# Two cross attentions on one core: one stored row for an item's columns and keys, and norms stored by item

## The chip, the core and the metric

The kernel runs on 1 core of a Trainium2 chip. Its engines, each with its own instruction stream, are PE (TensorE), DVE (VectorE), ACT (ScalarE), POOL (GpSimd) and SP, which here only issues transfers. The transfers of all streams run on 16 DMA engines. The metric is the device time in microseconds (us) of one execution, start to end; before and after are compared by the medians of several runs.

## The reference, cut to what matters

Two layers work on `x` (64 items of 32 rows of 256); each is a cross attention, a self attention and a mixture of experts, each added to `x`. Both cross attentions read the same context `ctx_1024` (64 items of 257 keys of 128). The second one normalizes queries and keys:

```
def _L1_xattn_ref(hidden_states, encoder_hidden_states, Wq, Wk, Wv, Wo, gq, gk):
    ...
    q = rmsnorm(q, gq)
    k = rmsnorm(k, gk)
    scores = jnp.einsum('bqhd,bkhd->bhqk', q, k) * scale
    attn = jax.nn.softmax(scores, axis=-1)
    out = jnp.einsum('bhqk,bkhd->bqhd', attn, v)
    out = out.reshape(B, Sq, H * D)
    return out @ Wo
```

There are 16 heads of 128. The norm of a key differs by head and key, so for an item it is 16 x 257 numbers.

## The kernel before

The stages follow each other, each in its own block: `begin`, `cross_attention` with layer 0 (some 60 to 580 us of the profile), `self_attention`, `routed_experts` (made of `route`, `experts` and `bridge`, up to some 1375 us), `cross_attention` with layer 1 (to some 2230 us), then the second layer's self attention and experts.

**Cross attention.** The weights of queries and keys are folded, so that an item's scores are one product of `qT` with the item's context columns (`ctxT`, context turned to 128 x 257), and the mix is a product of the probabilities with the context rows (`keys`, 2 blocks of 128 keys), from which the item's last, 257th key has been subtracted (`last_key`), since its share follows from the others. An outer iteration covers 8 items (`NB`), each 4 steps (`R`) of 4 heads; there are 8 iterations. In step s PE turns the probabilities of step s, makes the scores of step s+4 (`AHEAD`) and mixes step s-3 (`LAG`). DVE multiplies scores by `key_scale` and takes the maximum (L750), makes `shift` (L754), and divides by the sum (L765, L766); ACT takes the exponential (L637) and keeps the turned probabilities (L645). Between iterations PE makes the next queries.

**Layer 0** loads the rows of an item 8 items ahead (`ROWS`), POOL subtracts the last key (`less_last`, L891) into a ring of 4 (`RING`), and PE turns the rows into `ctxT`, which stays on the chip.

**The norms of the keys** (`KeyNorms`) are made beside `route`, `experts` and `bridge`: PE multiplies 128 keys at a time by the key weights, ACT and DVE sum squares, and groups of 512 keys are turned and stored in the DRAM tensor `rk`, a row of 16448 + 512 numbers for each head, four copies. In `experts` ACT issues these stores, in `bridge` SP. `route` also stores `ctxT` in the DRAM tensor `ctx_cols`, in 8 pieces, since its place on the chip is needed.

**Layer 1** takes for each item: the columns (L431), the keys (L432), the last key copied to all partitions (L434), and the scales in 4 transfers, one for each step (L440). `columns`, `keys` and `last_key` are rings of 4, filled when the item four before is mixed; `key_scale` has two buffers. All these are issued by SP in the order in which they are written, so a wait holds up what stands behind it. The wait before L440 lets the load for item b go when item b-2 has been scored. POOL subtracts the last key here too, then issues 16 gathers (L947) in four quarters at items 3 to 6: rows of the experts' output that DVE adds to `x` in the next iteration (`take`, L783). Between the first and the second quarter stands `norm_scale` (L871, L872), which makes `rstd` for the next iteration; DVE's `normalize` (L717), which stands right behind the first score of item 5, waits for it. After each of the first four iterations SP issues three loads of codes (L1997) for the following self attention, before the last iteration 16 loads of scales (L2007).

## Time and profile before

| | us |
|---|---|
| median of 3 runs | 3126.5 |
| lowest and highest | 3115.49 and 3131.35 |
| the profiled execution, its own time | 3116.77 |
| its span, first to last instruction | 3115.0 |
| PE busy | 2820.8 (91%) |
| DVE, ACT, POOL busy | 1478.4, 1352.8, 743.7 |
| mean granted PE clock | 0.957 |

The profile is one execution; its times are taken from the span's start. PE is the busiest engine. A busy share over the whole span mixes stages with different limits, so it is read by stretch. Registers, waits and issues of transfers don't count as busy. A wait is put down to what came last before the instruction started.

### The profile page before, as it was taken

How to read it: one execution, taken by the hardware profiler on the slowest of the kernel's cores; microseconds unless marked ns; L12 is line 12 of the kernel's file. 1: busy time of each engine (PE TensorE's matmuls, PEld its weight loads, DVE VectorE, ACT ScalarE, POOL GpSimd, SP SyncE). 2: the span in 40 equal slices, each digit the busy share in tenths (PEclk: the TensorE clock that was granted, in tenths of full speed). 3: DMA queues.
4: the chain of work that ended last, by engine and by line, in shares of the span. 5: the costliest groups of instructions: out<-in, count | busy, mean ns of one | idle time of the engine just before them, and what ended most of it. 6: DMA issues, size and time to landing. Idle time of an engine off the chain costs nothing. (4 is left out here: it accounts for less than half of the span.)

```text
span 3115.0 us, 50339 instructions
## 1 busy us (share of the span) xinstructions
PE 2820.8 (91%) x13964; PEld 2112.3 (68%) x13964; DVE 1478.4 (47%) x4967; ACT 1352.8 (43%) x4875; POOL 743.7 (24%) x948
## 2 busy tenths in 40 slices
PE   6999999798999899867887887798799999997999
PEld 5888888686444444345664665566678888885888
DVE  3665556465776444435435534543433333332333
ACT  2555455465666566524334334433422222221333
POOL 1332223263555000233322313223320000000000
PEclk9999999899999999988988999999899999998999
DMA  4110000202500243125246335525520000000000
GB/s 151 29 28 23 20 23 13 84 0 94 197 2 1 87 119 109 45 69 132 55 96 124 73 77 101 104 55 109 127 62 0 0 0 0 0 0 27 7 10 10
DMA packets 190907, 176.28 MB, mean 57 GB/s; under 512 B 32348, under 2 KB 171033, under 8 KB 189107
## 3 DMA queue, kind: packets, MB, share of 16 engines
q1 hardware_dynamic: 167762, 143.95, 16.3%
q0 software_dynamic: 14592, 27.33, 5.5%
q10 hardware_dynamic: 8416, 3.57, 0.8%
q8 instruction: 39, 0.64, 0.1%
q14 instruction: 98, 0.79, 0.1%
HBM read 147.41 MB, written 39.90 MB: 60 GB/s over the span
## 5 line engine op out<-in xcount | busy, mean ns | idle before, releaser
L529 PE MATMUL xa_mix_ps<-xa_probsT,xa_keys 128*128 128x256 f32 x1024 | 322.0, 399 | 0.0
L509 PE MATMUL xa_score_ps<-xa_columns,xa_qT 128*128 128x257 f32 x512 | 183.8, 449 | 96.1 <-DVE xa_shift L754 73.6
L637 ACT ACTIVATE xa_probs<-xa_probs,xa_shift,xa_row_scale 128x257 f32<-128x257 f32 x256 | 153.7, 601 | 269.2 <-DVE xa_shift L754 243.1
L221 PE MATMUL rt_kn_key_ps<-moe_w_wk,all_big 128*128 128x512 f32 x560 | 253.4, 605 | 7.3 <-remote 4.6
L2084 PE MATMUL sa_work_ps<-sa_xnT,all_big 128*128 128x128 f32 x2048 | 237.0, 279 | 11.2 <-ACT sa_xnT L2154 5.7
L516 PE MATMUL xa_probsT_ps<-all_ident,xa_probs 128*128 128x128 f32 x1024 | 209.7, 288 | 40.4 <-ACT xa_probsT L645 17.4
L2084 PEld LDWEIGHTS sa_work_ps<-sa_xnT,all_big 128*128 128x128 f32 x2048 | 235.3, 196 | 12.0 <-ACT sa_xnT L2154 6.1
L496 PE MATMUL xa_misc_ps<-xa_xnT,cross_folded 128*128 128x256 f32 x1024 | 232.9, 382 | 6.2 <-ACT xa_squares L622 5.6
L645 ACT ACTIVATE xa_probsT<-xa_probsT_ps 128x256 f32<-128x256 f32 x512 | 188.4, 370 | 93.6 <-PE xa_probsT_ps L516 82.8
L538 PE MATMUL xa_misc_ps<-cross_folded,xa_mixT 128*128 128x256 f32 x1024 | 228.2, 379 | 0.0
L529 PEld LDWEIGHTS xa_mix_ps<-xa_probsT,xa_keys 128*128 128x128 f32 x1024 | 202.6, 203 | 29.7
L516 PEld LDWEIGHTS xa_probsT_ps<-all_ident,xa_probs 128*128 128x128 f32 x1024 | 137.9, 147 | 124.5 <-DVE xa_probs L766 49.0
L496 PEld LDWEIGHTS xa_misc_ps<-xa_xnT,cross_folded 128*128 128x128 f32 x1024 | 194.9, 191 | 39.6 <-ACT xa_squares L622 12.2
L538 PEld LDWEIGHTS xa_misc_ps<-cross_folded,xa_mixT 128*128 128x128 f32 x1024 | 194.6, 190 | 26.5
L766 DVE TENSOR_SCALAR xa_probs<-xa_probs,xa_share 128x257 f32<-128x257 f32 x512 | 198.6, 388 | 18.2
L221 PE MATMUL ex_kn_key_ps<-moe_w_wk,all_big 128*128 128x512 f32 x448 | 202.1, 594 | 0.7 <-DVE moe_kn_stats L270 0.7
L750 DVE CUSTOM_DVE_ANT_0 xa_probs<-xa_score_ps,xa_key_scale 128x257 f32<-128x257 f32 x256 | 107.9, 422 | 183.3 <-DMA xa_key_scale<-rk 77.9
L221 PEld LDWEIGHTS rt_kn_key_ps<-moe_w_wk,all_big 128*128 128x128 f32 x560 | 104.8, 193 | 130.6 <-issue 110.9
L242 ACT ACTIVATE rt_kn_key_ps<-rt_kn_key_ps 128x128 f32<-128x128 f32 x560 | 148.3, 265 | 91.9 <-PE rt_kn_key_ps L221 65.8
L637 ACT ACTIVATE xa_probs<-xa_probs,xa_top 128x257 f32<-128x257 f32 x256 | 130.0, 508 | 106.7 <-DVE xa_top L750 103.7
L509 PEld LDWEIGHTS xa_score_ps<-xa_columns,xa_qT 128*128 128x128 f32 x512 | 89.6, 214 | 122.2 <-DVE xa_shift L754 94.8
L509 PE MATMUL xa_score_ps<-all_big,all_spare 128*128 (+1 forms) x512 | 152.6, 385 | 1.4 <-issue 0.8
(309 smaller groups left out, 5241.8 us busy)
## 6 DMA issues: line engine op xcount, KB each, us to landing
xa_key_scale<-rk SPq DMA_DIRECT2D x256, 128.5 KB
ctx_cols<-all_big SPq DMA_DIRECT2D x8, 1028.0 KB
xa_columns<-ctx_cols SPq DMA_DIRECT2D x64, 128.5 KB
xa_rows<-in_ctx_dram SPq DMA_DIRECT2D x64, 128.0 KB, 2.2
xa_last_key<-in_ctx_dram SPq DMA_DIRECT2D x128, 64.0 KB, 3.0
xa_keys<-in_ctx_dram SPq DMA_DIRECT2D x64, 128.0 KB
cross_folded<-in_L_ffn_w_gate_dram SPq DMA_DIRECT2D x32, 192.0 KB, 2.5
cross_folded<-in_L_ffn_w_up_dram SPq DMA_DIRECT2D x32, 192.0 KB, 2.7
```

Of the source, the lines that this page charges most:

```text
L221: pe.matmul(self.key_ps[m % self.banks][0:n, :], self.ctxT[:, c * P:c * P + n], self.wk[:, q * 512:(q + 1) * 512], start=True, stop=True). ...
L242: ins = act.activation(keys, keys, ACT.Square, accum_out=self.sums[0:n, c, q * self.HQ + h:q * self.HQ + h + 1])
L496: ins = pe.matmul(misc_ps[hp % 2][:, j * N:(j + 1) * N], folded[:, 2 * hp + j, c * P:(c + 1) * P], xnT[:, c, :], start=(c == 0), stop=(c = ...
L509: pe.matmul(score_ps[s % 2][:, 0:S2], qT[:, b, r * HR:(r + 1) * HR, :].rearrange("p h t -> p (h t)"), columns[:, b % RING, :] if layer els ...
L516: ins = pe.transpose(probsT_ps[s % 2][:, k * P:(k + 1) * P], probs[:, s % SR, k * P:(k + 1) * P], ident[:, :])
L529: ins = pe.matmul(mix_ps[b % 2][:, cols], keys[:, b % RING, k, :], probsT[:, b % 2, k, cols], start=(k == 0), stop=(k == KB - 1))
L538: ins = pe.matmul(misc_ps[t][:, 0:D], mixT[:, h, t * P:(t + 1) * P], folded[:, h, NC * P:FOLDED], start=(h == 0), stop=(h == H - 1))
L637: act.activation(probs[:, s % SR, :], probs[:, s % SR, :], ACT.Exp, bias=least, scale=scale, accum_out=total[:, col]).then_inc(exped, 1)
L645: act.activation(probsT[:, b % 2, :, r * P:(r + 1) * P], probsT_ps[s % 2][:, 0:KB * P].rearrange("p (k n) -> p k n", k=KB), ACT.Copy).then ...
L750: ins = dve.tensor_tensor_reduce(out=probs[:, s % SR, :], in0=score_ps[s % 2][:, 0:S2], in1=other, scale=1.0, scalar=start, op0=op, op1=pi ...
L766: dve.tensor_scalar(probs[:, s % SR, :], probs[:, s % SR, :], share[:, col], None, ALU.mult).then_inc(probs_ready, 1)
L2084: ins = pe.matmul(ps[:, j, :], w[:, c, h * HD:(h + 1) * HD], xnT[:, c, :], start=(c == 0), stop=(c == NC - 1))
```

## The change

In layer 0 SP also stores, for each item, its columns and its keys less the last in one row for each partition of a new DRAM tensor `pairs` (513 numbers, 2052 B). Layer 1 loads that row in one transfer into a ring `pair`, of which `columns` and `keys` are parts; POOL's subtraction there, `last_key` and `ctx_cols` go. The tensor `rk` is laid out by item, copy, head and key; heads are ordered so that the 4 heads which a block of 32 partitions needs follow each other, and L440 becomes 4 loads of 32 partitions with rows of 4 x 257 numbers (4112 B). A group of 512 keys belongs to up to 3 items, so its store becomes up to 3 transfers: 77 in `experts` instead of 26, 19 in `bridge` instead of 7. In layer 1, POOL waits before each quarter of the gathers until the items before it are mixed. The loads of codes move from behind an iteration's 8 items to behind its items 1, 3 and 5.

```
-RK_AHEAD = GROUP
 RK_COPIES = 4
+PAIR = S2 + (S2 - 1) // P * DC
...
+    def parts(self, j):
+
+        a, b = self.groups[j]
+        start, stop = a * P, min(b * P, KEYS)
+        return [(item, max(start, item * S2), min(stop, (item + 1) * S2)) for item in range(start // S2, (stop - 1) // S2 + 1)]
+
+    def stores_to(self, j):
+
+        return sum(len(self.parts(k)) for k in range(j % 2, j, 2))
+
     def store(self, sp, j):
-        a, b = self.groups[j]
-        n = min(b * P, KEYS) - a * P
+        start = self.groups[j][0] * P
         sp.wait_ge(self.rk_kept, j + 1)
-        sp.dma_start(self.rk_dram.rearrange("(h c) n -> h c n", c=RK_COPIES)[:, :, RK_AHEAD + a * P:RK_AHEAD + a * P + n],
-                     self.rkT[:, j % 2:j % 2 + 1, 0:n].broadcast_to([H, RK_COPIES, n])).then_inc(self.rk_stored[j % 2], 16)
+        for item, first, stop in self.parts(j):
+            sp.dma_start(self.rk_dram[item, :, :, first - item * S2:stop - item * S2].rearrange("c h s -> h c s"),
+                         self.rkT[:, j % 2:j % 2 + 1, first - start:stop - start].broadcast_to([H, RK_COPIES, stop - first])
+                         ).then_inc(self.rk_stored[j % 2], 16)
...
+                def store(item, b):
+
+                    sp.wait_ge(ctx_kept, item + 1)
+                    to = pairs[bass.ds(item, 1), :, :].rearrange("a p n -> p (a n)")
+                    sp.dma_start(to[:, 0:S2], ctxT[:, bass.ds(item * S2, S2)]).then_inc(columns_stored, 16)
+                    sp.wait_ge(keys_ready, item + 1)
+                    sp.dma_start(to[:, S2:PAIR], keys[:, b % RING, :, :].rearrange("p k d -> p (k d)")).then_inc(keys_stored[b % RING], 16)
...
-                        sp.wait_ge(keys_ready, item + 1)
+                        store(item, b)
...
+            def items(i, codes=False):
                 for b in range(NB):
                     item = i * NB + b
                     sp.wait_ge(mixed, item + 1)
-                    sp.dma_start(columns[:, b % RING, :], ctx_cols[:, bass.ds(item * S2, S2)]).then_inc(keys_loaded[b % RING], 16)
-                    sp.dma_start(keys[:, b % RING], ctx_in[bass.ds(item, 1), 0:KB * P, :].rearrange(
-                        "a (k p) d -> p (a k) d", p=P)).then_inc(keys_loaded[b % RING], 16)
-                    sp.dma_start(last_key[:, b % RING, :], ctx_in[bass.ds(item, 1), KB * P, :].broadcast_to([P, DC])
+                    sp.dma_start(pair[:, b % RING, :], pairs[bass.ds(item, 1), :, :].rearrange("a p n -> p (a n)")
                                  ).then_inc(keys_loaded[b % RING], 16)
                     sp.wait_ge(shifted, item * R)
-                    for r in range(R):
-                        src = rk_dram[r * HR * RK_COPIES:(r + 1) * HR * RK_COPIES,
-                                      bass.ds(item * S2 + RK_AHEAD, S2)]
-                        sp.dma_start(key_scale[:, b % 2, r, :], src.unsqueeze(1).broadcast_to(
-                            [HR * RK_COPIES, T // RK_COPIES, S2])).then_inc(kscale_loaded[b % 2], 16)
+                    for j in range(HR):
+                        src = rk_dram[bass.ds(item, 1), :, j * R:(j + 1) * R, :].rearrange("a c r s -> (a c) (r s)")
+                        sp.dma_start(key_scale[j * T:(j + 1) * T, b % 2, :, :].rearrange("p r s -> p (r s)"),
+                                     src.unsqueeze(1).broadcast_to([RK_COPIES, T // RK_COPIES, R * S2])
+                                     ).then_inc(kscale_loaded[b % 2], 16)
+                    if codes and b % 2 and b < NB - 1:
+                        after.load_codes(sp, ("wq", "wk", "wv")[b // 2], i, codes_ahead)
 
             for g in range(SA_GROUPS):
-                items(g)
-                for name in ("wq", "wk", "wv"):
-                    after.load_codes(sp, name, g, codes_ahead)
+                items(g, codes=True)
...
+                        if layer == 0:
+                            pe.wait_ge(keys_ready, i * NB + b + 1)
...
-                ring = RING if layer else ROWS
-                pool.wait_ge(keys_loaded[b % ring], i * (LOADS * NB // ring) + LOADS * (b // ring + 1))
-                if layer == 0:
-                    pool.wait_ge(mixed, i * NB + (b + 1))
+                pool.wait_ge(keys_loaded[b % ROWS], i * (LOADS * NB // ROWS) + LOADS * (b // ROWS + 1))
+                pool.wait_ge(mixed, i * NB + (b + 1))
+                pool.wait_ge(keys_stored[b % RING], i * (16 * NB // RING) + 16 * (b // RING + 1))
                 apart(pool, pool_passed)
-                pool.tensor_tensor(keys[:, b % RING], keys[:, b % RING] if layer else rows[:, b % ROWS],
-                                   last_key[:, b % ring, :].unsqueeze(1).broadcast_to([P, KB, DC]), ALU.subtract
+                pool.tensor_tensor(keys[:, b % RING], rows[:, b % ROWS], last_key[:, b % ROWS, :].unsqueeze(1).broadcast_to([P, KB, DC]), ALU.subtract
                                    ).then_inc(keys_ready, 1)
...
                     if b == ROW_STATS // R + 1 and not last:
                         norm_scale(i + 1, link)
                     if layer == 1 and not last and FIRST_GATHER <= b < FIRST_GATHER + 4:
+                        pool.wait_ge(mixed, i * NB + (RING + b))
+                        apart(pool, pool_passed)
                         if b == FIRST_GATHER:
                             next_places(i + 2)
                         gather(b - FIRST_GATHER)
...
-            for n in range(PIECES):
-                keys = slice(n * KEYS // PIECES, (n + 1) * KEYS // PIECES)
-                eng.dma_start(ctx_cols[:, keys], ctxT[:, keys]).then_inc(loaded, 16)
...
-            rk_dram = nc.dram_tensor("rk", (H * RK_COPIES, RK_AHEAD + KEYS), F32).ap()
+            rk_dram = nc.dram_tensor("rk", (B, RK_COPIES, H, S2), F32).ap()
...
+            pairs = nc.dram_tensor("pairs", (B, P, PAIR), F32).ap()
```

On SP, in layer 1 (`xa1`), the last item of one of the first four iterations and the loads of codes behind it; before:

```order
L431 DMA xa1_columns<-ctx_cols 128x257
L432 DMA xa1_keys<-in_ctx_1024_dram 128x2x128
L434 DMA xa1_last_key<-in_ctx_1024_dram 128x128
L440 DMA xa1_key_scale<-rk 128x1x257 x4
L1997 DMA all_big<-in_L1_attn_wq_codes_dram 128x2x512
L1997 DMA all_big<-in_L1_attn_wk_codes_dram 128x2x512
L1997 DMA all_big<-in_L1_attn_wv_codes_dram 128x2x512
```

Now, items 1 to 3 of such an iteration:

```order
L463 DMA xa1_pair<-pairs 128x513
L468 DMA xa1_key_scale<-rk 32x1x1028 x4
L2023 DMA all_big<-in_L1_attn_wq_codes_dram 128x2x512
L463 DMA xa1_pair<-pairs 128x513
L468 DMA xa1_key_scale<-rk 32x1x1028 x4
L463 DMA xa1_pair<-pairs 128x513
L468 DMA xa1_key_scale<-rk 32x1x1028 x4
L2023 DMA all_big<-in_L1_attn_wk_codes_dram 128x2x512
```

Seven issues for an item have become five, and the codes stand between items instead of behind all eight.

On POOL, in layer 1, the places, the first quarter of the gathers and what follows it; before:

```order
L939 COPY xa1_places<-cross_slots 128x16
L947 DMA all_big<-slot_out,xa1_places 128x256 x4
L887 REGISTER_ALU
L891 TENSOR_TENSOR xa1_keys<-xa1_keys,xa1_last_key 128x256
L871 TENSOR_SCALAR xa1_rstd<-xa1_mv 128x2
L46 ISA
L872 TENSOR_TENSOR xa1_rstd<-xa1_rstd,xa1_minus_half 128x2
L947 DMA all_big<-slot_out,xa1_places 128x256 x4
```

and now:

```order
L967 ISA
L969 ISA
L969 COPY xa1_places<-cross_slots 128x16
L977 DMA all_big<-slot_out,xa1_places 128x256 x4
L901 TENSOR_SCALAR xa1_rstd<-xa1_mv 128x2
L46 ISA
L902 TENSOR_TENSOR xa1_rstd<-xa1_rstd,xa1_minus_half 128x2
L953 REGISTER_ALU
L977 DMA all_big<-slot_out,xa1_places 128x256 x4
```

The subtraction is gone; `rstd` still stands between the first and the second quarter. The waits for mixed items stand ahead of the copy of the places and at L953.

On SP, in layer 0 (`xa0`), one item; before:

```order
L422 DMA xa0_rows<-in_ctx_1024_dram 128x2x128
L424 ISA
L424 DMA xa0_last_key<-in_ctx_1024_dram 128x128
L420 REGISTER_ALU
L422 ISA
```

and now:

```order
L439 DMA pairs<-all_big 128x257
L441 ISA
L441 DMA pairs<-xa0_keys 128x256
L449 ISA
L449 DMA xa0_rows<-in_ctx_1024_dram 128x2x128
L451 ISA
L451 DMA xa0_last_key<-in_ctx_1024_dram 128x128
```

Two stores stand ahead of the two loads of each item.

## Rows read from the trace of the kernel before

**Rows 1.** Busy time by stretch: us, engines with counts, clock, DMA share, GB/s.

```profile
60.00:560.00 500.00, 496.86 (x2595) 426.86 (x2593) 289.42 (x1170) 276.54 (x866) 149.17 (x200) 1.00 0.08 22
1410.00:1700.00 290.00, 229.47 (x890) 163.46 (x888) 146.35 (x572) 118.68 (x330) 87.69 (x115) 0.88 0.51 104
1700.00:2120.00 420.00, 345.28 (x1394) 247.19 (x1393) 200.71 (x761) 166.73 (x453) 125.23 (x173) 0.94 0.42 86
```

**Rows 2.** Waits, 1410 to 2220 us: us in total, times, longest.

```profile
DVE xa_probs L750 <- DMA xa_key_scale<-rk: 77.9, 15, 13.3
...
POOL xa_keys L891 <- DMA xa_last_key<-in_ctx_dram: 193.8, 20, 18.5
...
PE xa_score_ps L509 <- DVE xa_shift L754: 73.6, 60, 8.9
...
PE xa_score_ps L509 <- DMA xa_last_key<-in_ctx_dram: 8.9, 5, 2.4
```

**Rows 3.** Timeline of ACT, once an iteration: start, duration, work.

```profile
1477.03 0.60 ACT L615 ACTIVATE xa_xnT<-xa_misc_ps 128x512 f32<-128x512 f32 x1 [0.50 <-PE xa_misc_ps L465]
...
1701.78 0.60 ACT L615 ACTIVATE xa_xnT<-xa_misc_ps 128x512 f32<-128x512 f32 x1
...
1809.46 0.60 ACT L615 ACTIVATE xa_xnT<-xa_misc_ps 128x512 f32<-128x512 f32 x1
...
2129.79 0.60 ACT L615 ACTIVATE xa_xnT<-xa_misc_ps 128x512 f32<-128x512 f32 x1
```

**Rows 4.** Timeline of DVE: item 4, item 5 with its normalize, item 7.

```profile
1772.33 0.43 DVE L750 CUSTOM_DVE_ANT_0 xa_probs<-xa_score_ps,xa_key_scale 128x257 f32<-128x257 f32 x1
...
1780.63 0.43 DVE L750 CUSTOM_DVE_ANT_0 xa_probs<-xa_score_ps,xa_key_scale 128x257 f32<-128x257 f32 x1 [2.38 <-issue]
...
1781.28 0.74 DVE L717 TENSOR_SCALAR xa_xn<-all_x,xa_mv,xa_rstd 128x256 f32 x2
...
1802.75 0.43 DVE L750 CUSTOM_DVE_ANT_0 xa_probs<-xa_score_ps,xa_key_scale 128x257 f32<-128x257 f32 x1 [6.72 <-DMA xa_key_scale<-rk]
```

**Rows 5.** Timeline of SP in the last iteration.

```profile
2190.79 2.48 SPq L440 DMA_DIRECT2D xa_key_scale<-rk  x4
...
2195.81 2.47 SPq L440 DMA_DIRECT2D xa_key_scale<-rk  x4
2198.65 0.33 SPq L431 DMA_DIRECT2D xa_columns<-ctx_cols  x1
2199.03 0.43 SPq L432 DMA_DIRECT2D xa_keys<-in_ctx_dram  x1
2199.50 0.47 SPq L434 DMA_DIRECT2D xa_last_key<-in_ctx_dram  x1
2200.45 2.58 SPq L440 DMA_DIRECT2D xa_key_scale<-rk  x4
```

**Rows 6.** DMA queues, 2182 to 2205 us: packets, MB, share of 16 engines.

```profile
DMA packets 5124, 3.99 MB, mean 173 GB/s; under 512 B 512, under 2 KB 5120, under 8 KB 5120
...
q1 hardware_dynamic: 5120, 3.95, 58.5%
```

**Rows 7.** The same, 1783 to 1800 us; q0 carries the gathers.

```profile
DMA packets 1789, 2.14 MB, mean 126 GB/s; under 512 B 269, under 2 KB 1536, under 8 KB 1789
...
q0 software_dynamic: 378, 1.04, 59.8%
q1 hardware_dynamic: 1411, 1.10, 27.5%
```

**Rows 8.** The same, 773 to 785 us.

```profile
q1 hardware_dynamic: 693, 5.04, 101.9%
```

**Rows 9.** The same, 1369 to 1373 us.

```profile
q1 hardware_dynamic: 80, 0.02, 2.0%
```

**Rows 10.** The same, 2146 to 2151 us.

```profile
q1 hardware_dynamic: 532, 0.88, 51.8%
```

**Rows 11.** Timeline of SP at the loads of scales.

```profile
2144.73 1.77 SPq L2007 DMA_DIRECT2D all_spare<-in_L_attn_wq_scales_dram  x4
```

**Rows 12.** Timeline of PE: the last mix of item 2 and what follows.

```profile
1773.98 0.59 PE L529 MATMUL xa_mix_ps<-xa_probsT,xa_keys 128*128 128x256 f32 x2
```

**Rows 13.** Timeline of POOL: places, two of the gathers, subtraction, `rstd`.

```profile
1767.47 0.25 POOL L939 COPY xa_places<-cross_slots 128x16 uint32 x1 [17.40 <-DVE all_x L783]
...
1771.41 1.00 POOL L947 DMA_INDIRECT all_big<-slot_out,xa_places  x1 [0.30 <-issue]
1772.71 1.00 POOL L947 DMA_INDIRECT all_big<-slot_out,xa_places  x1 [0.30 <-issue]
1773.73 0.74 POOL L891 TENSOR_TENSOR xa_keys<-xa_keys,xa_last_key 128x256 f32<-128x256 f32 x1
...
1774.80 0.74 POOL L872 TENSOR_TENSOR xa_rstd<-xa_rstd,xa_minus_half 128x2 f32<-128x2 f32 x1
```

**Rows 14.** Timeline of SP: the scales of items 2 and 4.

```profile
1742.58 2.47 SPq L440 DMA_DIRECT2D xa_key_scale<-rk  x4
...
1766.36 2.47 SPq L440 DMA_DIRECT2D xa_key_scale<-rk  x4
```

**Rows 15.** DMA share in tenths, 1743 to 1748 us in 40 slices.

```profile
DMA  0000000546962466688788443689889866776544
```

**Rows 16.** DMA queues, 1310 to 1330 us: only gathers.

```profile
q0 software_dynamic: 743, 2.05, 35.6%
```

**Rows 17.** Busy time by stretch, in `route`.

```profile
800.00:1000.00 200.00, 198.69 (x561) 94.39 (x560) 148.34 (x704) 136.75 (x888) 113.98 (x129) 1.00 0.11 37
```

**Rows 18.** Timeline of ACT in `experts`: a store of norms and the next square.

```profile
1142.57 0.58 ACTq L306 DMA_DIRECT2D rk<-ex_kn_rkT  x1
1144.20 0.26 ACT L242 ACTIVATE ex_kn_key_ps<-ex_kn_key_ps 128x128 f32<-128x128 f32 x1 [1.27 <-PE ex_kn_key_ps L221]
```

58 lines of the change are left out of this document (34 added, 24 removed).

## The prediction

> **What bounds the kernel now.** I read the busy shares by stretch first. In the first cross attention (60 to 560 us) PE is busy 99% at full clock; in the second (1410 to 2120 us) it is busy 79 to 82%, at a granted clock of 0.88 and 0.94, while the DMA share is 0.51 and 0.42 instead of 0.08 [rows 1]. So the second cross attention has time to give, the first has none. Then the waits of that stretch: DVE waits 77.9 us in 15 places for `key_scale`, POOL 193.8 us for `last_key`, and PE's 73.6 us of waiting for `shift` follow DVE's [rows 2]. Then the period: the step L615 comes once in each outer iteration, six of them take 2129.79 - 1477.03 = 652.8 us, 108.8 each; one takes 1809.46 - 1701.78 = 107.7 [rows 3]. I call S4, S5, ... the moments at which DVE starts the scores of items 4, 5, ... of an iteration (8 items in it). In this one S4 is 1772.33 and S7 is 1802.75: 30.4 us for three items [rows 4]. In the last iteration, which has no gathers, the issues for one item after another start at 2190.79, 2195.81 and 2200.45: 4.6 to 5.0 us an item [rows 5]. Undisturbed, three items take 13.8 us, so that iteration would take 107.7 - 30.4 + 13.8 = 91.1, and the mean excess is 108.8 - 91.1 = 17.7 us: S4 to S7 is 31.5 us in the mean. Seven iterations have gathers: some 120 us in all, the most that the change can win.
>
> **Why items 5 to 7 are late.** `key_scale` has two buffers, so the load for item b is issued when item b-2 has been scored. Four issues take 2.47 us [rows 5]; with three more the SP queue spends about 3.9 us on each item. Without gathers the engines move 173 GB/s at a share of 0.585 [rows 6]. With gathers the share of the gathers is 0.598 and that of the loads 0.275, together 0.87, but only 126 GB/s [rows 7]: the engines are full, and the loads queue.
>
> **Part 1, the new `key_scale` load.** It moves the same bytes: 4 transfers for an item, each 32 partitions by 4112 B, instead of 128 by 1028 B. Engine time for a long row: the window with rows of 8224 B moved 5.04 MB in 12 us at a share of 1.019, so 5.04 MB / (12 x 16 x 1.019) = 25.8 kB/us for an engine [rows 8]; 4112 B are 0.16 us. For short rows: 3.95 MB / (23 x 16 x 0.585) = 18.3 kB/us [rows 6], 0.22 us. I take 0.16, since the row is longer than any of that window.
> How many engines share it decides the rest, and no row shows it directly. A transfer of 64 short rows has 80 packets, 16 more, one for each engine [rows 9]: that one used all. The loads of the scales also have 32 partitions; while they ran alone, issued every 0.46 us, the share stood at 0.518 [rows 10, 11], though more had been issued than was served: about half of the engines. The new load's source has as its outermost dimension only 4 rows, each read by 8 partitions (before: 16 rows). I estimate 4 engines, and the same four for all four transfers. Then each of these moves 32 rows an item: 32 x 0.16 = 5.1 us, and its 8 rows of the pair, 8 x 0.08 = 0.6 us: 5.7 us an item against the 4.6 it may take. With 8 engines it is 3.2, with 16 engines 1.9 us.
> The Trainium skill, "DMA: Bandwidth & Descriptors", section "Why a DMA increments its semaphore by 16 and not by 1", says that the number of engines is the largest up to 16 that divides the slowest dimension of both sides, and that a hardware queue takes the lowest-numbered ones. By that rule the new load gets 4, always the same, and the old one 16; the scales would get 16, where [rows 10] show half. So rule and row disagree on one load, and what it gives here is the forecast.
>
> **Part 2, one load for columns and keys.** Before: 128 rows of 1028 B, 256 of 512 B and 128 of 512 B, 3 issues. Now 128 of 2052 B, 1 issue. It takes about 1.0 us of SP per item, 64 KB, and 384 packets away. It is the only part that helps at any engine count. POOL's subtraction (0.74 us, 64 times) goes too; it lay beside other work: the matmuls L529 did not wait for it. PE's 8.9 us for `last_key` [rows 2] are inside the 120.
>
> **Part 3, the gathers wait.** POOL no longer waits for keys but, before each quarter of the gathers, until items 0 to b-1 are mixed; the first quarter starts only when item 2 is mixed. That is PE's mix near 1774.6, about S4 + 2.2 [rows 12], where POOL began at S4 - 4.9 [rows 13]. Behind the first quarter on POOL stands `norm_scale`, for which DVE's normalize (L717) waits. From the copy of the places to the end of `rstd` it is 1775.54 - 1767.47 = 8.1 us [rows 13], less 0.74 for the subtraction and with 0.6 to wake: 8.0. So `rstd` is there at S4 + 10.2, while DVE asks for it 0.65 us after S5 [rows 4]. If item 5 comes as early as S4 + 5.5, DVE stands 4 us, with ACT's exponentials and PE's turns behind it. This is a new wait in each of 7 iterations.
>
> **The sum with 4 engines.** Item 4: its load is issued at 1766.36 and used at 1772.33, 6.0 us later [rows 4, 14]; now it needs 1.4 us to the first packet (1742.58 to 1743.9 [rows 14, 15]), 5.1 and some 0.4 to finish, 6.9: it is 0.9 us later. Item 5's load starts at S4 + 0.9 behind that of item 4, and the gathers begin at S4 + 3.9: with some 0.8 for them, S5 = S4 + 6.8. Gathers alone: 35.6% of 20 us for 2.05 MB, 15.7 gathers of 131 kB, 0.45 us of all engines each [rows 16]; among loads 0.598 x 17 / 7.9 = 1.29 us each [rows 7]. POOL issues one every 1.31 us [rows 13].
> At 0.45 the gathers take a third, a load needs 5.1 / 0.66 = 7.7 us. Item 6's starts at S4 + 7.5: S6 = S4 + 15.3 (DVE's stall ends at 10.2 and item 5 at 14.3, hidden behind this). Item 7's is issued at 14.3, starts at 16: S7 = S4 + 24. Gain 31.5 - 24 - 0.9 = 6.6 us.
> At 1.29 the turns between queues halve the speed: S6 = S4 + 18.5, S7 = S4 + 28.6. Gain 2.0 us.
> Seven iterations: 46 or 14 us. The last iteration loses, 5 items x (5.7 - 4.6) = 5.5 us. Sum: -41 or -9. I take the middle, **-25 us**, since rows four times as long interleave less often, but the gathers are the same.
>
> **Parts that I cost at nothing.** The first cross attention gets 2 more issues an item on SP and 257 KB of stores; SP waits there for `ctx_kept` and `keys_ready`, which it needed anyway, four issues are about 1.6 us of 7.6, PE is 99% busy and DMA 8% [rows 1]. Were PE to wait for a load, 64 items times each tenth of a us would be 6.4 us. POOL's wait for the stored keys lies four items, some 30 us, behind the store. The 8 stores of `ctx_cols` go, under a PE that is 99% busy (1.00 clock) [rows 17]. The norms' store becomes 77 issues on ACT instead of 26, up to three in a row: 3 x 0.58 = 1.75 us from 1142.57, to 1144.3, where ACT's next work starts at 1144.20 after 1.27 us of idling [rows 18]; 0.1 us late, then it waits for PE again. If none were hidden: 51 x 0.58 = 30 us. The split addition L291 is 9 short instructions. The code loads move into items 1, 3 and 5: 1.3 us of engines each, the one behind item 5 may cost item 6 some 0.7 us in 4 iterations; in the range.
>
> **The rivals.**
> Rival A, all (or half the) engines share the load: nothing is late but DVE's new wait. S7 = S4 + 5.5 + 4.6 + 4.6 + 4.0 = 18.7; gain 12.8 x 7 = 90 us. For it: 128-partition loads spread well. Against: the half share of the scales. Time 3126.5 - 90 = 3036.
> Rival B, the gathers' inflation stays whole and the codes add to it: -9 to 0, time 3117 to 3126.
> Rival C, slower: the four engines get only the short-row speed, 0.22 us a row: 7.0 + 0.6 = 7.6 us an item. The last iteration loses 5 x 3.0 = 15, item 4 comes 2.8 us later, S4 to S7 is 3 x 7.6 / 0.66 = 34.5: each iteration loses 5.8, 41 us; in all +56, 3182. It decides from about 0.19 us a row, where S4 to S7 reaches 31.5 less the later item 4.
> That the change wins nothing because items 5 to 7 were bound by something else: against it, DVE's named waits.
>
> **The numbers.** The sum was made against the profiled execution, 3116.8 us (span 3115.0); the median of the runs shown is 3126.5, 9.7 more, and I set the change against that: 3126.5 - 25 = **3101**. Its own range is 3085 to 3118. Chances: forecast 0.57, rival A 0.15, B 0.17, C 0.11. The range of 3036 to 3142 takes in A's middle and leaves out most of C. A measurement tells about 0.5%, 15.6 us, from no change. Faster by more (under 3111): most of the forecast, all of A: 0.63. Within: the rest of it and B: 0.26. Slower: 0.11.
>
> **What would show it.** Right: DVE's waits for `key_scale` stay in items 5 to 7 and appear in the last iteration, where issues come 5.7 us apart; the DMA share while only such loads run is near 0.25 with high waits; `xn` waits for `rstd` about 3 us, seven times; POOL shows no L891-like work. Wrong: a share above 0.5 in the last iteration and no wait for `key_scale` (A); issues over 7 us apart there (C); PE under 95% busy in the first cross attention, or ACT ahead of PE's norms, would put a cost where I put none.

## The result, and the profile after

The changed kernel takes 3139.4 us (median of 11 runs), the kernel before 3123.3 us (11 runs beside them): ratio 1.0047, 95% interval 1.0029 to 1.0064. It is slower by 0.5%, where 25 us less were forecast and 3036 to 3142 us were allowed. That the time lies inside that wide range is no merit of the forecast: the change was to make the kernel faster and made it slower, for which the prediction had a chance of 0.11. The profiled execution of after has a span of 3141.6 us against 3115.0. I cut both by DVE's scores in the second cross attention: from the first to the last of them it takes 826.9 us, before 796.4, so 30.5 more; all the rest of the program takes 3.9 less. The two profiled executions lie 26.6 us apart, the medians 16; what follows explains the 30.5.

Three rows of busy time by stretch (us, engines with counts, TensorE's clock, DMA share, GB/s), to be held against [rows 1]:

```profile
60.00:560.00 500.00, 496.86 (x2594) 427.44 (x2593) 289.31 (x1168) 274.80 (x861) 149.50 (x200) 1.00 0.20 54
1410.00:1700.00 290.00, 227.96 (x907) 159.18 (x906) 144.93 (x572) 121.51 (x340) 71.39 (x93) 0.93 0.45 102
1700.00:2120.00 420.00, 343.64 (x1349) 250.33 (x1348) 195.16 (x739) 158.28 (x432) 98.12 (x139) 0.90 0.35 74
```

The first cross attention stores its pairs under a PE that is as busy as before, to the hundredth: 496.86 us. In the second the engines move less (DMA share 0.35 instead of 0.42) and yet PE is not busier. The waits, 1410 to 2220 us (total us, times, longest), against [rows 2]:

```profile
PE xa_score_ps L538 <- DVE xa_shift L784: 97.4, 62, 8.4
DVE xa_probs L780 <- DMA xa_key_scale<-rk: 88.9, 29, 9.1
POOL all_big L977 <- PE xa_mix_ps L559: 66.5, 15, 9.0
...
DVE xa_xn L747 <- POOL xa_rstd L902: 14.3, 7, 3.6
```

DVE's wait for `key_scale` has grown from 77.9 us in 15 places to 88.9 in 29: shorter waits, at more items (93.1 us in 31 places up to the end of the stage, which now lies behind 2220 us; before it stays at 77.9 in 15). `rstd` is waited for seven times, as predicted. DVE's first score of each of five items in one iteration (start, duration, work, the idle time before it and what ended it):

```profile
1858.14 0.43 DVE L780 CUSTOM_DVE_ANT_0 xa_probs<-xa_score_ps,xa_key_scale 128x257 f32<-128x257 f32 x1 [4.59 <-issue]
...
1873.61 0.43 DVE L780 CUSTOM_DVE_ANT_0 xa_probs<-xa_score_ps,xa_key_scale 128x257 f32<-128x257 f32 x1
...
1881.33 0.43 DVE L780 CUSTOM_DVE_ANT_0 xa_probs<-xa_score_ps,xa_key_scale 128x257 f32<-128x257 f32 x1 [3.14 <-DMA xa_key_scale<-rk]
...
1898.28 0.43 DVE L780 CUSTOM_DVE_ANT_0 xa_probs<-xa_score_ps,xa_key_scale 128x257 f32<-128x257 f32 x1 [1.80 <-DMA xa_key_scale<-rk]
...
1911.98 0.43 DVE L780 CUSTOM_DVE_ANT_0 xa_probs<-xa_score_ps,xa_key_scale 128x257 f32<-128x257 f32 x1 [9.13 <-DMA xa_key_scale<-rk]
```

These are items 1, 3, 4, 6 and 7. Item 4 comes 7.7 us after item 3 and waits for its load, which in the kernel before it did only in the last iteration. From such rows, the mean of iterations 2 to 7, the time from one item's first score to the next one's:

| us | to item 1 | 2 | 3 | 4 | 5 | 6 | 7 | to the next iteration | period | last iteration |
|---|---|---|---|---|---|---|---|---|---|---|
| before | 15.0 | 7.5 | 8.4 | 4.7 | 9.1 | 11.6 | 10.9 | 41.6 | 108.8 | 44.2 |
| after | 17.0 | 7.5 | 8.6 | 7.4 | 7.2 | 11.0 | 9.7 | 43.2 | 111.6 | 58.3 |

"To the next iteration" counts from item 7's first score, "last iteration" from its first score to its last. Items 5 to 7 did win, 3.7 us in all. Item 4 lost 2.7, item 1 lost 2.0 and the stretch between iterations 1.6. Seven iterations: 16.4 us lost; the last one loses another 14.1.

### The profile page after: what moved, and what is told of

Same layout as the page of the kernel before. It is cut to its first block and busy times, and to the rows that moved or that the text cites. A ratio compares the mean times of both kernels' runs of the same rounds, so it can differ in the third digit from the quotient of the medians.

```text
span 3141.6 us, 50358 instructions
## 1 busy us (share of the span) xinstructions
PE 2827.8 (90%) x13964; PEld 2119.4 (67%) x13964; DVE 1477.2 (47%) x4976; ACT 1352.2 (43%) x4875; POOL 695.8 (22%) x884
## 5 line engine op out<-in xcount | busy, mean ns | idle before, releaser
L538 PE MATMUL xa_score_ps<-xa_pair,xa_qT 128*128 128x257 f32 x512 | 189.5, 461 | 110.0 <-DVE xa_shift L784 99.9
L796 DVE TENSOR_SCALAR xa_probs<-xa_probs,xa_share 128x257 f32<-128x257 f32 x512 | 197.6, 386 | 18.2
L780 DVE CUSTOM_DVE_ANT_0 xa_probs<-xa_score_ps,xa_key_scale 128x257 f32<-128x257 f32 x256 | 108.1, 422 | 189.2 <-DMA xa_key_scale<-rk 93.1
L538 PEld LDWEIGHTS xa_score_ps<-xa_pair,xa_qT 128*128 128x128 f32 x512 | 93.3, 222 | 135.4 <-DVE xa_shift L784 122.8
L559 PE MATMUL xa_mix_ps<-xa_probsT,xa_pair 128*128 128x256 f32 x512 | 172.6, 423 | 0.0
L242 ACT ACTIVATE ex_kn_key_ps<-ex_kn_key_ps 128x128 f32<-128x128 f32 x448 | 118.6, 265 | 80.1 <-PE ex_kn_key_ps L221 80.0
```

The source lines that it names most:

```text
L242: ins = act.activation(keys, keys, ACT.Square, accum_out=self.sums[0:n, c, h * self.NQ + q:h * self.NQ + q + 1])
L538: pe.matmul(score_ps[s % 2][:, 0:S2], qT[:, b, r * HR:(r + 1) * HR, :].rearrange("p h t -> p (h t)"), columns[:, b % RING, :] if layer els ...
L559: ins = pe.matmul(mix_ps[b % 2][:, cols], keys[:, b % RING, k, :], probsT[:, b % 2, k, cols], start=(k == 0), stop=(k == KB - 1))
L796: dve.tensor_scalar(probs[:, s % SR, :], probs[:, s % SR, :], share[:, col], None, ALU.mult).then_inc(probs_ready, 1)
```

## Which engines carry the load

The runs were made on four chips, each beside the kernel before: e1 to e4 on one, e5 to e8 on the next, then e9 and e11 to e13, then e14 to e16. So ratios to before are compared, and within one group also the times.

**Run e1, all engines.** In the changed kernel the source of a `key_scale` transfer runs over 4 copies, and inside each over 8 repetitions. One edit turns this round, so that the outermost dimension has 16:

```
-    src = rk_dram[item, :, j*R:(j+1)*R, :]        -> (a c) (r s)
-    src.unsqueeze(1).broadcast_to([RK_COPIES, T // RK_COPIES, R * S2])
+    src = rk_dram[item, 0:2, j*R:(j+1)*R, :]      -> (a c) (r s)
+    src.unsqueeze(0).broadcast_to([T // 2, 2, R * S2])
```

> The changed kernel, with one edit: in the source of the key_scale load the repetition is now the outermost dimension (16 repetitions of 2 copies) instead of 4 copies with 8 repetitions in each; bytes, rows of 4112 B, issues and everything else are as in the changed kernel (3139 us). My theory, that the load was served by four of the 16 DMA engines, always the same: DVE then waits for key_scale only between gathers. The last iteration, 58.3 us from its first to its last score, comes to 44 (-14). In each of the seven iterations with gathers item 4 comes 2.7 us earlier, items 5 to 7 together take between 18.7 (only the new wait for rstd is left) and 24 us instead of 28, and what was added at item 1 and at the iteration's end (about 1.6 and 2 us) goes if the code of the engines was loaded behind those rows, and stays if not. Sum 60 to 125 us less: 3015 to 3080. Rival, that rows of 4112 B read again and again from the same few rows of DRAM are slow for any number of engines: no more than the last iteration's half, 3125 to 3139. Rival, that the gathers alone hold items 5 to 7: the last iteration, item 4 and the ends come back, 14 + 7 x 4.5, some 45 us, 3095. By the rule of the Trainium skill ('DMA: Bandwidth & Descriptors', section 'Why a DMA increments its semaphore by 16 and not by 1') the new outermost dimension of 16 gives 16 engines.

Measured: 3062.7 us, 0.983 of before (0.981 to 0.985), some 67 us less than the changed kernel by the ratios; the stage, from DVE's first score to its last, takes 742.0 us instead of 826.9. The bytes, rows and issues are the same. Two copies are read instead of four; the next run reads four.

**Run e2, eight engines.** The same with `unsqueeze(0)` and all 4 copies: 8 repetitions of 4.

> The same as the run with 16 repetitions, but with 8 repetitions of 4 copies as the source's outermost dimensions: the same bytes and rows. My theory (the outermost dimension sets how many engines work): eight engines, a load of an item takes about 2.8 us instead of 5.6. The last iteration comes to 44 to 46 us, the DMA share while only these loads run may rise to 0.5, and items 5 to 7 stand between the run with 16 and the changed kernel: 40 to 110 us less than the changed kernel's 3139, and 0 to 20 more than the run with 16. Rival (the number of copies read matters, not the engines): four copies are as good as or better than two, time at or below the run with 16.

Measured: 3066.0 us, 0.985 (0.982 to 0.987). The queue that carries the loads (packets, MB, share of 16 engines), in 3 us of the last iteration in which it carries next to nothing but `key_scale`; first the changed kernel (2203 to 2206 us), then e2 (2149 to 2152 us):

```profile
q1 hardware_dynamic: 87, 0.30, 26.7%
```

```profile
q1 hardware_dynamic: 144, 0.47, 45.3%
```

A quarter of the engines' time, then nearly half: four engines that never rest, and eight that rest for a tenth of it. 0.30 MB in 3 us is 100 GB/s, 0.47 is 157. In e1 such a stretch (2135.7 to 2138 us) reads, with the DMA share in tenths in 40 slices above it:

```profile
DMA  0000000095699933552100000000081595873329
...
q1 hardware_dynamic: 102, 0.29, 37.1%
```

The mean share is *less*, though in some slices over nine tenths of the 16 engines work, which four or eight cannot reach: each issue brings 2 rows to an engine, and between the transfers there are stretches in which nothing moves. So a half share in the mean does not show that half the engines are in use. By the Trainium skill, "DMA: Bandwidth & Descriptors", section "Why a DMA increments its semaphore by 16 and not by 1", the number of engines is the largest up to 16 that divides the outermost dimension on both sides; 4, 8 and 16 here. The trace agrees with it (26.7%, 45.3%, and slices above nine tenths), and so do the last iterations: 58.3, 48.0 and 43.6 us.

DVE's first scores of items 3, 4, 5 and 7 in that iteration of the changed kernel, and below them of items 4, 6 and 7 in e1:

```profile
2203.29 0.43 DVE L780 CUSTOM_DVE_ANT_0 xa_probs<-xa_score_ps,xa_key_scale 128x257 f32<-128x257 f32 x1 [5.04 <-DMA xa_key_scale<-rk]
...
2210.20 0.43 DVE L780 CUSTOM_DVE_ANT_0 xa_probs<-xa_score_ps,xa_key_scale 128x257 f32<-128x257 f32 x1 [1.50 <-DMA xa_key_scale<-rk]
...
2217.77 0.43 DVE L780 CUSTOM_DVE_ANT_0 xa_probs<-xa_score_ps,xa_key_scale 128x257 f32<-128x257 f32 x1 [3.00 <-DMA xa_key_scale<-rk]
...
2231.73 0.43 DVE L780 CUSTOM_DVE_ANT_0 xa_probs<-xa_score_ps,xa_key_scale 128x257 f32<-128x257 f32 x1 [3.18 <-DMA xa_key_scale<-rk]
```

```profile
2135.32 0.43 DVE L780 CUSTOM_DVE_ANT_0 xa_probs<-xa_score_ps,xa_key_scale 128x257 f32<-128x257 f32 x1
...
2145.03 0.43 DVE L780 CUSTOM_DVE_ANT_0 xa_probs<-xa_score_ps,xa_key_scale 128x257 f32<-128x257 f32 x1
2149.66 0.43 DVE L780 CUSTOM_DVE_ANT_0 xa_probs<-xa_score_ps,xa_key_scale 128x257 f32<-128x257 f32 x1
```

With four engines every item waits for its load; with 16 none of these does, and items 7 and 6 stand 4.63 us apart.

## The wait for rstd and the gathers' pace

**Run e3**: on POOL, `norm_scale` stands ahead of the first quarter of the gathers, four engines.

> The changed kernel, with norm_scale moved on POOL ahead of the places and the first quarter of the gathers in layer 1. Its waits for rstd, 14.3 us in 7 places on DVE, go. My theory: most of that lay ahead of item 6, whose load is late anyway, so the gain is 0 to 5 us: 3134 to 3139, no difference that can be told. Rival: DVE's stand is on the path, with PE's turns and ACT behind it, and all of it comes back: 3125.

Measured: 3140.6 us, 1.008 (1.006 to 1.010). The wait for `rstd` is gone, the wait for `key_scale` is 96.9 us instead of 88.9, the period stays 111.6. Taking one wait away moved it to the next. Against e1, on the same chip, it is 78 us slower.

**Run e4**: the changed kernel without the pace, POOL's wait ahead of each quarter of the gathers: the line `pool.wait_ge(mixed, i * NB + (RING + b))`.

> The changed kernel without the wait of the gathers for the mixed items: POOL issues all 16 as soon as the rows of the iteration before are taken. The wait for rstd goes, the gathers run under items 2 to 5 instead of 4 to 7, and none is left when the iteration ends. My theory: the gathers then slow the loads of items 3 to 5, and free those of 6 and 7; the sum moves by -15 to +10 us (3124 to 3149). If the stretch from the last score to the next iteration's first (39.3 us in the mean, before 37.5) was lengthened by the last gathers, it comes back to 37.5, if by the key_scale load it stays. Rival: the pace was worth what it was put there for, and without it the loads of early items, which have no reserve either, push the time up by more than 15 us.

Measured: 3181.2 us, 1.021 (1.019 to 1.023): 1.6% slower than the changed kernel by the ratios, 1.3% slower than e3 on the same chip. My own interval, 15 us either way, was wrong: I had counted the new wait only as a cost. DVE now waits 110.0 us for `key_scale`, and item 6 takes 15.3 us instead of 11.0.

**Run e5**: e1 and e3 together.

> The kernel with 16 repetitions of 2 copies (0.983 of the kernel before, 3063 us), with norm_scale ahead of the places and the first quarter of the gathers on POOL, as in the run where this alone was changed. There DVE waits 27.7 us in 7 places for rstd, and item 6 comes 9.9 us after item 5. Theory: now nothing but this wait holds item 6, so it comes back, less what the load of item 6 then lacks: its last packets are served about 7 us after item 5's first score, so item 6 can come 2 to 3 us earlier, and item 7's load then meets the gathers. 7 to 20 us less, 3043 to 3056. Rival: all 28 us come back, 3035. Rival: as with the four engines, nothing, since item 7 gives it back: 3063.

Measured: 0.974 (0.973 to 0.976). **Run e12** is the same kernel on another chip:

> The run with 16 engines and norm_scale first once more, on the chip of the other three, so that they can be compared with it: 0.974 of before, since chips differ by 1% in the time of the kernel before (3080 to 3123 us so far).

Measured: 0.979 (0.977 to 0.982). By the ratios that is 0.4 to 0.9% faster than e1, 13 to 28 us, where 7 to 20 were expected; against e7 (below; the chip of e5, and a row length that turns out not to matter) e5 is 15 us faster. Item 6, 9.9 us in e1, takes 7.2 in e5 and 9.0 in e12. The same kernel gives chips different gains; why is open.

**Run e6**: e1 without the pace.

> The kernel with 16 repetitions of 2 copies, without the wait of the gathers for the mixed items. With four engines on the load the same edit cost 42 us. Theory: it costs less here, since a load is served in a third of the time, but gathers under items 1 to 5 still delay these loads, which have no reserve: 5 to 30 us more, 3068 to 3093. Rival: with all engines on the load the pace is not needed; the wait for rstd (27.7 us) goes as well, and the time falls to 3040 to 3063.

Measured: 0.995 (0.994 to 0.997), 1.2% slower than e1, or 38 us, and 49 us slower than e7 on the same chip: above the upper end of my 5 to 30. **Run e8**: e5 with the pace one item earlier.

> As the run with norm_scale first, but each quarter of the gathers waits for one mixed item less, so it starts about one item earlier. Theory: the stretch between the last score and the next iteration's first, 38.8 us in the mean, comes back to 37.5 as in the run without the pace (-9 us in seven iterations), and the load of item 5 meets the first quarter (+0 to 3 us in each): -9 to +12 us against that run. Rival: the later the gathers the better for the scores, as with four engines, where no pace at all cost 42 us: +12 to +30.

Measured: 0.974 (0.973 to 0.976), equal to e5. Waiting for one item more or less does not matter, not waiting at all does (e4, e6).

**Run e11**: the kernel before with that one wait added.

> The kernel before with one edit: the four quarters of its gathers wait for the mixed items as in the changed kernel. Theory: there the gathers began 4.9 us ahead of item 4's first score, now 2 us behind it, so the load of item 5 is freed and those of 6 and 7 are hit instead, and DVE waits for rstd some 4 us in each iteration: -25 to +5 us, ratio 0.992 to 1.0015. Rival: the pace alone is what made the runs with 16 and 8 engines faster than before (without it, 0.995), so it is worth 1% here too: 0.985 to 0.99.

Measured: 0.989 (0.986 to 0.992). The rival is nearer. DVE's waits in the kernel before, with the pace:

```profile
DVE xa_xn L717 <- POOL xa_rstd L872: 32.6, 7, 4.7
DVE xa_probs L750 <- DMA xa_key_scale<-rk: 30.5, 10, 8.0
```

47 us less than in [rows 2] for the scales, 33 us of it lost again at `rstd`. Item 5 comes after 5.5 us instead of 9.1, item 7 after 8.8 instead of 10.9.

## Row length and the pair

**Run e7**: as e1, but `key_scale` has 258 elements a row, so that a transfer consists of rows of 1028 B, from one copy with 32 repetitions outermost.

> The kernel with 16 engines, but the four rows of 1028 B of a partition land in rows padded by one element, so that a transfer consists of rows of 1028 B (32 repetitions of one copy; the run with 8 repetitions of 4 copies showed that the number of copies does not matter). The same bytes, four times the packets. Theory: a row of 4112 B takes 0.18 us alone, four of 1028 B 4 x 0.054 = 0.22, so all engines are busy 1.7 instead of 1.4 us with an item, and among gathers a row waits for its turn four times as often: item 6 and 7 come 1 to 3 us later each, +10 to +40 us, 3073 to 3103. Rival: the row length is worth nothing, all of the gain is in the one transfer for columns and keys and in the gathers' pace: within 8 us of 3063.

Measured: 0.979 (0.977 to 0.980), not slower than e1's 0.983 but slightly faster, on another chip. **Run e13** settles it on the chip of e12:

> The run above with rows of 1028 B instead of 4112 B in the key_scale load, on the same chip. Theory after the run with short rows (0.979, where the same with long rows had 0.983 on another chip): the row length is worth nothing once 16 engines share the load, within 0.3% of the run above. Rival, the first idea of the change: with norm_scale no longer in the way the loads of items 6 and 7 are what counts, and rows four times as long let them through 0.5 to 1 us sooner each: 7 to 14 us, 0.2 to 0.45% slower than the run above.

Measured: 0.976 (0.974 to 0.979) beside 0.979 (0.977 to 0.982). The period is 100.7 and 100.9 us. Rows four times as long, the idea of the change, are worth nothing here once all engines share the load. That e7 and e13 read one copy 32 times and are no slower, and that e2 reads four, also shows that the copies in DRAM do not matter.

**Run e15**: e7 without the pace, so the one transfer for columns and keys by itself.

> The one transfer for columns and keys without the rest: rows of 1028 B on all engines as before, no pace for the gathers, norm_scale behind the first quarter as before. The kernel before with the pace alone had 0.989, pace and pair together with such rows 0.979, and the pair with rows of 4112 B and no pace 0.995. Theory: the pair is worth what is left, 0.5 to 1%, from 384 packets and two issues less for an item: 0.990 to 0.996. Rival: without the wait for the keys that used to hold up POOL the gathers all start with items 1 and 2, and the pair alone gains nothing: 0.997 to 1.01.

Measured: 0.993 (0.991 to 0.995). The pair is worth 0.7%, the pace 1.1% (e11), both together 2.1% (e7); these are three chips, so the sum need not close.

## The gathers out of the way

**Run e9**: e1, with POOL's order changed at the end of each iteration:

```
-    (items 3 to 6: wait for mixed items, one quarter of the gathers each)
+    next_places(i + 2)
+    pool.wait_ge(mixed, i * NB + (RING + NB))
+    gather(0); gather(1)
+    pool.wait_ge(gathered, ...)      # these two have landed
     row_scales(i + 1, link)
+    gather(2); gather(3)
+    pool.wait_ge(gathered, ...)
```

> The kernel with 16 engines on the load, with the gathers moved out of items 4 to 7: POOL copies the places and waits until the iteration's last item is mixed, issues two quarters, makes the row scales of the next iteration, and issues the other two quarters behind them. The engines move next to nothing in that stretch of 37 us. norm_scale, no longer behind a gather, is free. Theory (items 6 and 7 are late only because their loads share the engines with gathers): they come after 4.6 to 5.5 us instead of 7.3 and 7.9 (run with norm_scale first, 0.974 of before), 5 to 6 us less in each of seven iterations, some 38 us: ratio 0.962 to 0.965 of before. Rival: the last two quarters land only after DVE wants them in item 1 of the next iteration, or delay the row scales: 3 to 6 us more in each iteration, which eats the gain: 0.972 to 0.976.

Measured: 1.003 (1.001 to 1.004). Items 5 to 7 take 5.5, 5.1 and 4.7 us, as expected, and everything is lost between the iterations, 53.9 us from the last score to the next first one. POOL's first gather, and a wait of DVE's:

```profile
1823.41 1.14 POOL L979 DMA_INDIRECT all_big<-slot_out,xa_places  x1 [42.63 <-PE xa_mix_ps L559]
```

```profile
DVE xa_probs L780 <- POOL xa_row_scale L934: 139.2, 7, 21.4
```

The last score was at 1796.1: item 7's mix stands behind the query matmuls, 27 us later, and I had not looked at where. **Run e14** waits for item 6's mix instead (`RING + NB - 1`).

> The kernel whose first two quarters of gathers are issued between the iterations, with one number changed: POOL waits until item 6 is mixed, some 4 us after the last score, not item 7, whose mix stands behind the query matmuls, 27 us after it. There items 5 to 7 took 5.5, 5.1 and 4.7 us, but the row scales came late: 53.9 us from the last score to the next iteration's first instead of 37.5, and item 1 took 18.5 instead of 15. Theory: all 16.4 us of that go, and 3 us at item 1, since the last two quarters then land in time: a period of 91.5 us or less against 100.9 with the gathers under the items (0.979 of before). 7 x 9.4 or more: 65 to 95 us less than that, ratio 0.948 to 0.958. Rival: the row scales are still late, since POOL waits for the gathers to land before it makes them, or item 1 keeps its 3 us: 0.96 to 0.97.

Measured: 3004.3 us, **0.958** (0.955 to 0.960), the fastest of all by the ratio, faster than both kernels: 135 us less than before. One iteration of POOL and of DVE:

```profile
1737.78 1.14 POOL L979 DMA_INDIRECT all_big<-slot_out,xa_places  x1 [18.68 <-PE xa_mix_ps L559]
...
1759.02 4.63 POOL L934 TENSOR_SCALAR xa_row_scale<-xa_q_rms 32x8 f32<-32x8 f32 x16 [0.20 <-POOL xa_q_rms L930]
1764.53 1.13 POOL L979 DMA_INDIRECT all_big<-slot_out,xa_places  x1 [0.88 <-POOL xa_row_scale L934]
```

```profile
1806.97 0.43 DVE L780 CUSTOM_DVE_ANT_0 xa_probs<-xa_score_ps,xa_key_scale 128x257 f32<-128x257 f32 x1
...
1817.73 0.43 DVE L780 CUSTOM_DVE_ANT_0 xa_probs<-xa_score_ps,xa_key_scale 128x257 f32<-128x257 f32 x1 [0.31 <-PE xa_probsT_ps L545]
...
1822.48 0.43 DVE L780 CUSTOM_DVE_ANT_0 xa_probs<-xa_score_ps,xa_key_scale 128x257 f32<-128x257 f32 x1 [0.18 <-issue]
```

Items 4, 6 and 7: 15.5 us for the three steps that took 31.5 before. The period is 91.4 us, where the prediction had worked out 91.1 for an undisturbed one; that it comes so near is partly luck, since items 5 to 7 take 15.3 us in the mean instead of its 13.8, and the other steps 1.2 less than it had. The last iteration, 47.7 us, is 4 us longer than e1's; why is open.

**Run e16**: e14 with the changed kernel's load on four engines.

> The kernel with the gathers between the iterations and the sooner wait, but with the changed kernel's key_scale load on four engines. No gather is in the way of items 4 to 7, so this is the price of four engines by itself. Theory, from the changed kernel's last iteration, where items 3 to 7 took 9.3, 6.9, 7.6, 6.2 and 7.7 us instead of 4.6: a load takes 5.6 us for its own 32 rows an engine and is issued only when the item before last is scored, so items 4 to 7 take about 7 us each, 8 to 10 us more in each of eight iterations, and item 1 is 1.5 us longer as in the changed kernel: 75 to 95 us above the kernel with 16 engines, ratio about 0.975 to 0.985. Rival: much of the four engines' price came from the gathers that shared them, and here it is under 40 us.

Measured: 0.986 (0.984 to 0.988), 92 us above e14, 89.7 between the two stages. So the four engines cost about 90 us where no gather is in the way of items 4 to 7. With the gathers there it is 84.9 between the stages of e1 and the changed kernel, 78 between e1 and e3 on one chip (e3 also has `norm_scale` first), and 67 by the ratios of two chips; whether the gathers hide a part of the price is not clear from this. Items 4 to 7 take 7.3, 6.8, 7.9 and 6.3 us.

The means of iterations 2 to 7, as above:

| run | to item 1 | 4 | 5 | 6 | 7 | period | last iteration | ratio |
|---|---|---|---|---|---|---|---|---|
| e1 | 15.1 | 4.6 | 5.5 | 9.9 | 7.7 | 101.1 | 43.6 | 0.983 |
| e2 | 15.0 | 5.6 | 5.7 | 9.1 | 8.3 | 101.7 | 48.0 | 0.985 |
| e4 | 17.0 | 8.4 | 9.7 | 15.3 | 8.0 | 116.0 | 58.0 | 1.021 |
| e6 | 15.1 | 4.7 | 8.6 | 6.9 | 13.3 | 105.8 | 43.5 | 0.995 |
| e7 | 15.1 | 4.6 | 5.5 | 10.0 | 7.8 | 99.8 | 43.3 | 0.979 |
| e11 | 15.0 | 4.6 | 5.5 | 11.0 | 8.8 | 105.3 | 44.0 | 0.989 |
| e14 | 15.1 | 4.7 | 5.5 | 5.1 | 4.7 | 91.4 | 47.7 | 0.958 |
| e16 | 18.0 | 7.3 | 6.8 | 7.9 | 6.3 | 103.3 | 57.1 | 0.986 |

## Why the prediction was wrong, step by step

- **What bounds the kernel, and the most there is to win: right.** 120 us were put on the gathers and loads in each other's way; e14 with both out of the way wins 118 us in that stage (796.4 - 678.3).
- **How many engines carry the new load: the number was right, the way to it was not.** Four, and the same four for one transfer after another, since the share stays at a quarter while several have been issued. But the step from the scales' share of 0.518 [rows 10] to "about half of the engines" was unsound. e1 shows a mean of 37% with 16 engines, and the kernel before itself shows the same scales on more than half of them: from 2151.6 to 2153 us, with no other load running, the queue reads

```profile
q1 hardware_dynamic: 261, 0.43, 108.0%
```

  (packets overlap a little, so the share can pass 100%). So rule and row did not disagree: the rule of the skill, which I set aside for the scales, contradicts no load here. e7's loads, with 32 repetitions outermost, behave as those with 16.
- **The price of an item, 5.7 us against the 4.6 it may take: too small. This is one of the two steps that failed.** In the last iteration items came 7.1 us apart (2203.29 to 2231.73, 28.4 us for four steps; the step ahead of them took 9.3), and 6.8 in e16. The rows for items 4 to 7 run from 2202.7 to 2231.1 us, four loads in 28.4 us too; the DMA share in tenths and the queue:

```profile
DMA  2222228821122309682222222482212222112220
...
q1 hardware_dynamic: 1025, 2.92, 32.8%
```

  A 2 is four engines at work, higher digits are for the most part the pair's load, which runs on all, and at 1 fewer than four work. By the packets of the trace these 512 rows of 4112 B took 0.181 us in the mean, though half of them took 0.161 or less: 0.16 is what a row takes in a quiet stretch (26.7% of 16 engines for 3 us over about 77 rows is 0.166). One row in seven takes longer, up to 1.3 us, two thirds of these while the pair's rows run or right beside them. That makes 5.8 us of long rows an item instead of 5.1. And the four engines are busy for at most 92% of the time, so some 0.6 us an item goes idle, nearly half of it where one load runs out and the next was issued only a microsecond before: the load for an item is issued only when the item before last is scored. I added up the service time of one load by the price of quiet rows and took the queue to be always full. The last iteration was to lose 5.5 us and lost 14.1: rival C had 15 for it. Its reason, slow rows, holds in part (0.181 us where it had 0.22), and the rest of its sum, 56 us in all, does not.
- **Item 4, 0.9 us late: it was 2.7**, by the same price, in seven iterations 13 us more than forecast. In e1 it comes after 4.6 us again.
- **Items 5 to 7: right.** Forecast were 24 to 28.6 us for the three, measured 27.9, near the end at which gathers keep their inflation. The steps fit too: items 5, 6 and 7 come 7.2, 18.2 and 27.9 us after item 4, where that end had 6.8, 18.5 and 28.6.
- **Nothing was put on item 1 and on the stretch between iterations. This is the other step that failed**, 2.0 and 1.6 us, 24 us in seven iterations. At item 1 DVE stands 4.59 us with nothing to wait for in the profile ("issue"), before it was 3.17, in e1 2.99:

```profile
1859.72 0.43 DVE L750 CUSTOM_DVE_ANT_0 xa_probs<-xa_score_ps,xa_key_scale 128x257 f32<-128x257 f32 x1 [3.17 <-issue]
```

```profile
1819.80 0.43 DVE L780 CUSTOM_DVE_ANT_0 xa_probs<-xa_score_ps,xa_key_scale 128x257 f32<-128x257 f32 x1 [2.99 <-issue]
```

  The first is before, the second e1. In every run on four engines (after, e3, e4, e16) item 1 takes 17 to 18 us, in every other run but e9 15. So the load on four engines causes it. As to how, DVE is at the end of its loop there, and one packet of the queue for instructions (q14) falls into the stand. In all 17 traces, in each of iterations 2 to 7, this packet of 8192 B starts 2.2 to 2.5 us before item 1's first score, whether DVE stands 2.9 us or 6.6. What differs is how far into the stand it starts. The DMA share during the stand, in 40 slices, first the changed kernel (1853.55 to 1858.14 us), then e1 (1816.81 to 1819.80 us), where the single 4 is that packet:

```profile
DMA  7997513211312222121100000000000000000000
```

```profile
DMA  0000000004000000000000000000000000000000
```

  In the first the packet starts at 2.2 us, when the four engines are nearly through with a load, in the second at 0.7 us, with nothing ahead of it. In e9 (stands of 5.7 to 6.1 us) nearly all 16 engines are busy, mostly with gathers, until it starts. All this fits one reading: DVE waits for this packet, and the packet comes late where its engine is busy; e1 was expected to take the 2 us back if that was so, and did. No run moves the packet alone, so the reading is argued from the traces.

  The 1.6 us between iterations come from gathers that end late, with the pace. From an iteration's last score to the next first one it is 37.5 us in before and 40.5 in e11, which adds the pace; 37.6 in e6 and 38.8 in e1; 37.6 with four engines and no pace (e4), 39.3 in after.
- **The gathers' wait was costed only as a loss.** The stand of DVE at `rstd` is there (3.6 us at most, seven times; 2.0 in the mean; predicted about 3). But the pace itself is worth 1.1 to 1.6% (e11 against before, e4 against e3, e6 against e7, each pair on one chip). It is why the changed kernel loses no more than it does: in the prediction's sum its gain was hidden in the time at which the gathers begin.
- **What was costed at nothing outside the second cross attention: right**, the rest of the program is 3.9 us shorter.

The sum with the measured sizes: items 5 to 7 -3.7, item 4 +2.7, item 3 +0.3, item 1 +2.0, the stretch between +1.6, about +2.9 in each of six iterations; with the first iteration (-0.8) and the last (+14.1) it makes the 30.5. Between the 25 us less that were forecast and these 30.5 lie some 55. The price of an item makes 21 of them (item 4 13, the last iteration 9), the two places at which nothing was put 24, items 5 to 7 9, within their own range, and item 3 the rest.

## What to carry to other kernels

Look at the outermost dimension of both sides of a transfer before its row length: here the same bytes cost 67 to 92 us more on 4 engines than on 16, while rows of 4112 B instead of 1028 B were worth nothing. A load that comes near the time of its item is not served at the rate of a quiet stretch: here 5.7 us of work on four engines became 7.1, in about equal parts by rows slower than in the quiet stretch and by engines that stood idle. A wait that the profile calls "issue" at the end of a loop may be one for instructions that stand behind data. Where two streams share the DMA engines, move the one with slack into the stretch in which they rest, and look up first when the event that it waits for really happens: the same edit gave 1.003 with one wait and 0.958 with the wait one item sooner.

## What the runs showed of the hardware

- A repetition of the same rows, put outermost, counts like any other dimension: with 16 repetitions of 2 rows (e1) and 32 of one (e7) the last iteration takes 43.6 and 43.3 us, with 16 distinct rows in the kernel before 44.2, with 4 rows repeated inside 58.3.
- A share of the engines' time below one half does not tell how many work: 37% with 16, 45% with 8, 27% with 4; and the same loads of scales read 51.8% [rows 10] and, right behind that, 108.0%.
- DVE's first score of item 1 comes 2.2 to 2.5 us after a packet of the queue for instructions starts, in 102 iterations of 17 traces, however long it stood before.
- TensorE's granted clock, a mean over its two levels of 1.2 and 2.4 GHz where 1.00 is the upper, was 0.93 and 0.90 in the two stretches of the second cross attention in after, 0.88 and 0.94 before [rows 1]; in e14, where PE hardly waits, it was 0.99 in both:

```profile
1410.00:1700.00 290.00, 261.77 (x1118) 188.30 (x1116) 162.67 (x626) 134.25 (x369) 82.15 (x118) 0.99 0.47 107
1700.00:2050.00 350.00, 320.95 (x1368) 231.68 (x1369) 195.72 (x753) 166.32 (x457) 100.53 (x141) 0.99 0.49 101
```

  With PE's waits filled (261.77 us busy of 290 instead of 227.96) its clock was higher too.
- The same kernel, before, took 3080 us on one chip and 3114 to 3139 on the others, so only kernels of one chip, or ratios, can be compared. The kernel with 16 engines and `norm_scale` first had 0.974 of before on the first and 0.979 on another.
